# A Mamba2 block on one core: the odd tile's turned x taken from TensorE to VectorE and DRAM, its step size to ScalarE

## The reference, cut to what matters

```
xBC = silu(conv(xBC) + conv_b)          # depthwise, 4 taps
dt  = clip(softplus(dt + dt_bias), 0.001, 100)
cs  = cumsum(dt * A)                    # within a chunk
xdt = x * dt                            # per token and head
Ydiag  = einsum(scores, xdt)            # scores = (C B^T) * exp(cs_l - cs_s), lower triangle
states = einsum(B, exp(cs_last - cs), xdt)
```

## Time and profile before

| | us |
|---|---|
| median of 3 runs | 1759.31 (1758.42 to 1759.45) |
| the profiled execution, device time | 1758.21 |
| its span in the trace | 1756.4 |

### The profile page before, as it was taken

One profiled execution on the slowest core, in us unless ns is written; L12 is line 12 of the kernel. 1 busy time (PEld: TensorE's weight loads), 2 busy tenths in 40 slices (PEclk: granted clock), 3 DMA queues, 4 the chain that ended last, 5 costly groups with the idle time before them and its releaser, 6 DMA issues.

```text
span 1756.4 us, 30305 instructions
## 1 busy us (share of the span) xinstructions
PE 1742.4 (99%) x10301; PEld 1459.3 (83%) x10301; DVE 1402.7 (80%) x2211; ACT 1221.6 (70%) x2456; POOL 1232.1 (70%) x877
## 2 busy tenths in 40 slices
PE   8999999999999999999999999999999999999999
PEld 6788888888888888888888888888888888888877
DVE  7978788878878788778788788878887887868941
ACT  6986677777776777777867778767877787643320
POOL 5677777777876787677776777677777787576630
PEclk9999999999999999999999999999999999999999
DMA  5442333333333343333333333333323343236522
GB/s 196 165 131 99 116 116 112 98 123 109 134 105 94 104 135 109 108 101 117 118 102 118 116 111 108 103 109 127 123 91 103 109 135 107 76 98 175 146 78 96
DMA packets 122595, 202.84 MB, mean 115 GB/s; under 512 B 23056, under 2 KB 60560, under 8 KB 122192
## 3 DMA queue, kind: packets, MB, share of 16 engines
q1 hardware_dynamic: 120720, 197.32, 34.8%
q10 hardware_dynamic: 1728, 3.65, 0.5%
HBM read 193.57 MB, written 7.34 MB: 114 GB/s over the span
## 4 chain that ended last, share of the span: by engine, by line
PE 94%; DVE 3%; issue 1%; POOL 1%; DMA 0%; ACT 0%; SPq 0%; DVEq 0%; ACTq 0%; POOLq 0%
PE bank L143 17%; PE bank L145 16%; PE bank L144 16%; PE bank L573 10%; PE bank L609 7%; PE bank L677 7%; PE bank L679 7%; PE bank L678 6%; PE bank L888 3%; PE bank L738 3%; DVE z L1246 1%; PE bank L700 0%; DVE lm L1267 0%; PE bank L720 0%; DVE acc L1337 0%
## 5 line engine op out<-in xcount | busy, mean ns | idle before, releaser
L964 ACT ACTIVATE lm<-lm,hp 128x128 f32<-128x128 f32 x1024 | 313.1, 389 | 0.8
L1246 DVE SCALAR_TENSOR_TENSOR z<-bank,cw_all,z 128x511 f32<-128x511 f32 (+2 forms) x384 | 286.9, 747 | 13.3 <-ACT z L1000 4.2
L1611 POOL TENSOR_TENSOR conv_lo<-raw_x,conv_hi 128x512 fp32r<-128x512 f32 x124 | 203.7, 1643 | 129.4 <-ACT conv_hi L901 129.3
L143 PE MATMUL bank<-xn_hi,conv_hi 128*128 128x512 f32 x640 | 261.4, 408 | 1.9 <-DVE z L1246 1.4
L1306 DVE TENSOR_TENSOR xdt<-bank,hp 128x512 f32<-128x512 f32 x128 | 88.2, 689 | 212.4 <-PE bank L738 212.4
L145 PE MATMUL bank<-xn_hi,conv_lo 128*128 128x512 f32 x640 | 250.6, 392 | 0.0
L144 PE MATMUL bank<-xn_lo,conv_hi 128*128 128x512 f32 x640 | 249.5, 390 | 0.0
L1594 POOL TENSOR_TENSOR yt<-yt,ec 128x384 f32<-128x384 f32 x128 | 146.8, 1147 | 139.3 <-DVE ec L1315 107.9
L1280 DVE SCALAR_TENSOR_TENSOR lm<-lm,gm 128x1024 f32<-128x1024 f32 x128 | 225.3, 1760 | 7.8 <-ACT lm L964 7.2
L1578 POOL TENSOR_TENSOR y_lo<-yt,y_hi 128x512 fp32r<-128x512 f32 x128 | 180.1, 1407 | 52.4 <-ACT y_hi L1035 52.4
L143 PE MATMUL bank<-xn_hi,gate_hi 128*128 128x512 f32 x512 | 212.9, 416 | 0.0
(11 more groups left out here) (152 smaller groups left out, 4051.5 us busy)
## 6 DMA issues: line engine op xcount, KB each, us to landing
lm<-cs_d SPq DMA_DIRECT2D x128, 512.0 KB, 4.5
raw_x<-w_conv_dram SPq DMA_DIRECT2D x128, 256.0 KB, 3.5
ec<-e_d SPq DMA_DIRECT2D x256, 96.0 KB, 2.7
raw_o<-w_out_dram SPq DMA_DIRECT2D x64, 256.0 KB, 3.0
raw_g<-w_gate_dram SPq DMA_DIRECT2D x61, 256.0 KB, 3.2
raw_g<-w_conv_dram SPq DMA_DIRECT2D x16, 256.0 KB, 3.2
raw_o<-w_conv_dram SPq DMA_DIRECT2D x14, 256.0 KB, 3.4
q_raw<-w1q_dram SPq DMA_DIRECT2D x10, 256.0 KB, 3.9
```

The source lines that it names most:

```text
L143: pe.matmul(dst, a_hi, b_hi, start=(i == 0), stop=False)
L964: e = act.activation(lm[m % LM_BUFS][:, u, :], lm[m % LM_BUFS][:, u, :], ACT.Exp, bias=hp[bd.seq][:, Q_CS, k1, u:u + 1])
L1246: dve.scalar_tensor_tensor(dst[:, d:SEQ], src[:, 0:SEQ - d], cw_all[:, bd.group, pos, 3 - d:4 - d], dst[:, d:SEQ], ALU.mult, ALU.add).then ...
L1611: pool.tensor_tensor(conv_lo[kx % 2][:, :, :], raw_x[:, kx % 2, :].rearrange("p (k j) -> p k j", k=KT), conv_hi[kx % 2][:, :, :].bitcast(F ...
```

## The change

For the 59 odd tiles from 7 to 123 (`by_blocks`) x is no longer turned by TensorE. Two steps ahead VectorE transposes each 32x32 block of xt into `z[:, 1]`, SyncE writes that to a DRAM tensor `xb_d` (256 KB), and in the next step reads it back in four DMAs so that the blocks land in their turned places, in `xdt[1]`, in pieces of 32 floats. At step n VectorE makes `xw` from `xdt[1]`, and then ScalarE multiplies `xdt[1]` by dt in place, in eight operations of 128x64 with the step size as a scale per partition. `diag(n)` waits for that. Along with it `scores` of an odd step goes to the step's end, and the sum of squares of the last body from the end of step 0 to behind `y_off` of step 1.

```diff
+def by_blocks(t):
+    return paired(t) and t % 2 == 1 and t >= TILES - 1
 # SyncE
+            def blocks_out(t):
+                if by_blocks(t):
+                    sp.wait_ge(blk_done, blocks_before(t) + 1)
+                    wait(sp, xtok_in, 16 * BLK * blocks_before(t))
+                    sp.dma_start(xb_d.rearrange("g i c b j -> (g i) (c b j)"), z[:, 1, :]).then_inc(xb_out, 16)
+            def tokens_in(t):
+                if by_blocks(t):
+                    sp.wait_ge(xb_out, 16 * (blocks_before(t) + 1))
+                    sp.wait_ge(yd_done, t - 1)
+                    for b in range(BLK):
+                        sp.dma_start(xdt[1][32 * b:32 * b + 32, :].rearrange("i (c g j) -> i c g j", c=NC, g=BLK),
+                                     xb_d[:, :, :, b].rearrange("g i c j -> i c g j")).then_inc(xtok_in, 16)
                 load_rows(body, k)
+                blocks_out(n + 2)
                 ...                        # the two halves of ec
+                tokens_in(n + 1)
 # TensorE
             def diag(n, dst):
-                pe.wait_ge(xdt_done, n + 1)
+                if by_blocks(n):
+                    pe.wait_ge(xdt_act, blocks_before(n) + 1)
+                else:
+                    pe.wait_ge(xdt_done, n + 1 - blocks_before(n))
             def two_diags(body, k):
-                pe.wait_ge(xw_done, n + 1)
+                if by_blocks(n):
+                    pe.wait_ge(st_done, n)
+                else:
+                    pe.wait_ge(xw_done, n + 1)
             def turn_x(body, k):
-                if bd.exists():
+                if bd.exists() and not by_blocks(n + 1):
             def step(body, k):
                 y_off(body, k)
+                if k == 1 and body.exists():
+                    sum_squares(body, 0)
 # ScalarE
+            def weigh_x(body, k):
+                n = TILES * body.n + k
+                if by_blocks(n):
+                    act.wait_ge(xw_done, n + 1)
+                    for c in range(NC):
+                        for j in range(2):
+                            o = slice(c * P + HD * j, c * P + HD * j + HD)
+                            e = act.activation(xdt[1][:, o], xdt[1][:, o], ACT.Copy,
+                                               scale=hp[body.seq][:, Q_DT, k, NC * j + c:NC * j + c + 1])
+                    e.then_inc(xdt_act, 1)
             def raw_x_conv(body, k):
+                    if by_blocks(m - 2):
+                        act.wait_ge(xb_out, 16 * (blocks_before(m - 2) + 1))
                     work_a(body, k)
+                    weigh_x(body, k)
                     weights(body, k)
 # VectorE
+                    if by_blocks(n):
+                        dve.wait_ge(xtok_in, 16 * BLK * (blocks_before(n) + 1))
+                        dve.wait_ge(st_mm, n)
+                        dve.tensor_tensor(by_head(xw[:, :]), by_head(xdt[1][:, 0:(NC - 1) * P]),
+                                          per_token(hp[body.seq], Q_DEC, k, NC - 1), ALU.mult).then_inc(xw_done, 1)
+                    else:
                         ...                # xdt and xw from ps_x, as before
                 if pv.exists():
                     decayed()
+                if by_blocks(n + 2):
+                    dve.wait_ge(xs_done, n + 3)
+                    dve.transpose(z[:, 1, :], xt[:, (k + 2) % 4, :]).then_inc(blk_done, 1)
+                if k == 1 and before.exists() and body.exists():
+                    sums_by_token()
+                crowded = crowded or by_blocks(n)
```

More of the change, by code:

```diff
@@ L49 @@
 LM_BUFS = 4
+BLK = P // 32
 SH = 4
@@ L111, in paired, with blocks_before @@
     return TILES // 2 <= n < TILES * (BODIES - 1) + TILES // 2
+def by_blocks(t):
+    return paired(t) and t % 2 == 1 and t >= TILES - 1
+def blocks_before(t):
+    return sum(1 for u in range(t) if by_blocks(u))
 def group_exists(group):
@@ L166, in build @@
     hp_d = nc.dram_tensor("hp_d", (SEQS, P, NQ, GROUPS, TILES, 2 * NC), F32).ap()
+    xb_d = nc.dram_tensor("xb_d", (BLK, 32, NC, BLK, 32), F32).ap()
     mamba_d = nc.dram_tensor("mamba_d", (TT, P, DIM), F32).ap()
@@ L316, in build @@
         tx_done = sem("tx_done")
+        xdt_act = sem("xdt_act")
+        blk_done, xb_out, xtok_in = sem("blk_done"), sem("xb_out"), sem("xtok_in")
         xdt_done, xw_done = sem("xdt_done"), sem("xw_done")
@@ L711, in sum_squares @@
                     if body.exists():
-                        wait(pe, gev_done, TILES * body.n + k + 3)
+                        wait(pe, gev_done, TILES * body.n + 3)
                     else:
@@ L780, in step @@
                 turn_x(body, k)
-                sum_squares(body, k)
+                if not body.exists():
+                    sum_squares(body, k)
             def turn(t):
@@ L1288, in step, with sums_by_token @@
                 before = body.plus(-1)
-                if k == 1 and before.exists():
+                def sums_by_token():
                     dve.wait_ge(ss_mm, before.n + 1)
@@ L1298, in step, with decayed @@
                                       None, ALU.add).then_inc(rs_done, 1)
[L1300 to L1311, removed]
+                def decayed():
                     dve.wait_ge(yo_done, n)
@@ L1316, in step @@
                                       ).then_inc(t0_done, 1)
+                if k == 1 and before.exists() and not body.exists():
+                    sums_by_token()
+                if body.exists():
+                    if by_blocks(n):
[4 more added lines that the diff above has]
+                    else:
+                        dve.wait_ge(tx_done, n + 1 - blocks_before(n))
+                        if k == 0:
+                            wait_hp(dve, body)
+                        wait(dve, yd_done, n - 1)
+                        dve.tensor_tensor(by_head(xdt[n % 2][:, :]), by_head(ps_x[:, :]),
+                                          per_token(hp[body.seq], Q_DT, k, NC), ALU.mult).then_inc(xdt_done, 1)
+                        wait(dve, st_mm, n)
+                        dve.tensor_tensor(by_head(xw[:, :]), by_head(ps_x[:, 0:(NC - 1) * P]),
+                                          per_token(hp[body.seq], Q_DEC, k, NC - 1), ALU.mult).then_inc(xw_done, 1)
+                if pv.exists():
+                    decayed()
+                if by_blocks(n + 2):
+                    dve.wait_ge(xs_done, n + 3)
+                    dve.transpose(z[:, 1, :], xt[:, (k + 2) % 4, :]).then_inc(blk_done, 1)
+                if k == 1 and before.exists() and body.exists():
+                    sums_by_token()
                 if k == 0 and body.exists():
```

## The result

| | us |
|---|---|
| before, median of 4 runs | 1758.87 (1758.01 to 1759.45) |
| changed, median of 4 runs | 1849.83 (1847.37 to 1851.52) |
| ratio, 95% interval | 1.0514 (1.0501 to 1.0526) |
| the profiled execution, device time | 1850.88, span 1849.1 |

The change makes the kernel 91 us slower. The direction was forecast; 1811 was not, and 1850 lies outside of the range. The page's first part, against the earlier trace rows: TensorE's share falls from 99% to 95%, its busy time rises by 9 us though its stream has four transposes less in 59 tiles, and ScalarE has 112 us more.

What follows compares the result with a forecast made beforehand. TensorE, busy 99%, was taken as the bound, with ScalarE's stretch between its two waits deciding. Stalls net of removed transposes, 55.5 - 6.2 = +49, plus 3 for `scores`, gave +52 us: 1811 on the 1759.3 median; range 1788 to 1836.

Steps and rivals of the forecast that it cites:

- `diag(n)` would wait for ScalarE: By k, position of eight in a body: net +2.1 us at 3, +1.2 at 1, +0.4 at 7, -0.44 at 5.
- W: Length of ScalarE's eight `weigh_x` operations behind the exponentials: 1.97 us, taken as 2.0; bounds 1.0 and 2.45.
- the stalls of 0.84 and 1.64: TensorE's predicted waits ahead of `diag(n)` at k = 7 (0.84 us) and k = 1 (1.64 us).
- 2.55: TensorE's predicted stall ahead of `diag(n)` at k = 3, in us; net +2.1 with the transposes gone.
- The pairs of steps k = 0, 1 and 6, 7: Forecast change in length of these step pairs: +1.2 us and +0.4 us.
- Nothing was made up, nothing carried over: Claim that the stall is paid each time, as ScalarE's stretch starts anew from TensorE's clock in the next even step.
- the transpose: VectorE's 32x32 transpose, costed at nothing: between 0.69 and 1.76 us, taken as 0.7.
- signs of being wrong: Stall missing or at another k, VectorE's xw waiting for a DMA, or pairs that stall not stalling each time.
- a slide by `scores`: `scores` behind taps and state on VectorE delays the even step's chain into the k = 3 stall: 3 us (0 to 6).
- ScalarE's work behind `weigh_x` (rounding, conv copy) starts when `diag(n)` starts: Claim that this later ScalarE work adds no cost: same place at k = 3 today, 2.22 us idle later in that step.
- forecast signs: Expected in the profile after: among others, TensorE busy time down some 26 us, an eight-step body 3.3 us longer.

Runs made afterwards that it cites:

- fill_bc: Changed kernel with ScalarE's copy of C (k = 5) ahead of `weigh_x` and eight added TensorE matmuls in the k = 3 stall; 1810.33 us.
- fill_k3: Changed kernel with eight matmuls of 512 columns added at k = 3 between `diag(n-1)` and TensorE's wait for ScalarE; 1829.93 us.
- dve_weighs: Changed kernel, but VectorE multiplies `xdt[1]` by dt in one 128x512 operation behind t0 and ScalarE has no `weigh_x`; 1748.70 us.
- bc_first: Changed kernel with ScalarE's copy of the C projection (k = 5) put ahead of `weigh_x` instead of behind it; 1817.67 us.
- one_op: Changed kernel with one of ScalarE's eight multiplications by dt, seven left out; 1752.65 us.
- dve_early: dve_weighs with the four token reads issued ahead of the two ec loads of the same step instead of behind them; 1747.60 us.
- weigh_first: Changed kernel with `weigh_x` ahead of the exponentials of the same step instead of behind them; 1871.81 us.

## Why the prediction was wrong

Right: that `diag(n)` would wait for ScalarE, at k = 1, 3 and 7 and not at 5, and by how much. ScalarE's group takes 2.00 us (W was 1.97, taken as 2.0). The idle times in the middle of the pair are 0.63, 1.48 and 1.96 us by the trace (k = 7, 1, 3), 61 us in all; the stalls of 0.84 and 1.64 agree if the ends are taken by the start of the next group as in the working (953.06 - 951.33 - 0.95 = 0.78, and 977.38 - 974.80 - 0.95 = 1.63). At k = 3, 2.1 us lie in the middle and 0.3 ahead of the pair (it starts 0.64 us behind the last conv matmul, 0.32 before the change), since t0 is late behind an xw of 1.64 us; together 2.4 to 2.5, against 2.55. The pairs of steps k = 0, 1 and 6, 7 came to the forecast. Nothing was made up, nothing carried over; the transpose took 0.70 us. One of the signs of being wrong did appear: xw waits for the reads 15 times at k = 7, 22 us. It still ends 1.5 to 3 us before ScalarE starts on `weigh_x`, so it cost nothing. fill_bc, in which only this mechanism is left, takes 1810.3 against 1811. That it is so near is in part luck: 3 of the forecast's 52 us stood for a slide by `scores` that did not show, and by the pairs of steps the rest came out longer by as much.

Wrong, first: "ScalarE's work behind `weigh_x` (rounding, conv copy) starts when `diag(n)` starts. That is where it is at k = 3 today", costed at nothing. It was checked at k = 3 and taken over for all k. At k = 5 `diag(n)` does not wait for ScalarE, so everything behind `weigh_x` is simply 2 us later, and there `weights` holds the copy of C (the projection in step 4 that spares k = 5 is that of C, not of B as the prediction has it), which the gate projection needs in the same step through three taps of 2.3 us. Size: 1.4 us, 14 times, 19.6 us measured by fill_k3 against fill_bc. It was to be had from the kernel's own wait of the gate projection for the taps at k = 4 and 5.

Wrong, second: the sum took TensorE's matmuls at their length of the trace before, at full clock. After the idle time at k = 3, 2.0 us by the trace, they run at half clock, 1.5 us more in 14 bodies, 19.9 us measured by fill_k3. No rival stood for it. Before the change TensorE had no idle time of this length in the stretch, so its rows could not show what follows one; its clock was 1.000 over the whole span. The Trainium skill (TensorE: Matmul & The Clock Gate, Why this matters for your kernels) warns of idle gaps between bursts of matmuls, and was left out of the prediction; the gaps in which the clock fell here, 1.7 to 2.3 us in the changed kernel, are shorter than those that its table names.

The range went up to 1836. Its upper end held W and `scores` at their bounds, but no term for either of the two. Both were of the same kind: a consequence of the stall or of the longer ScalarE stretch outside of the chain that was worked out. Two of the forecast signs show them: TensorE's busy time went up by 9 us instead of down by 26 (in dve_weighs, with no half clock, down by 21), and a body became 6.4 us longer instead of 3.3.

Open: why the clock falls in 14 of 15 bodies of the changed kernel and in 5 of bc_first, whose stall at k = 3 is as long. In the paired steps of all ten traces the clock never fell without an idle time of at least 1.7 us beside it (fill_k3, fill_bc, one_op and dve_early have none and kept the clock). That is not enough: ten bodies of bc_first held it through the same stall, dve_weighs through one of 2.5 and weigh_first through one of 3.5. In the changed kernel the falls come 102.4 us apart, which is also the length of its body; whether that plays a part was not tried. What makes step 1 of dve_early long in every other body was seen in one timeline and not tried.

## What to carry to other kernels

An operation that is put into an engine's order delays all that stands behind it, and not only at the step where its own result is late: list each instruction behind it, in every kind of step, with who waits for it, above all where the step has slack, since there nothing masks the delay. A stall of TensorE costs more than its length if the clock falls in it; work that is thrown away can be cheaper than idleness. When an engine is 70% busy, read the stretch between its two waits for the bottleneck and not its share: VectorE at 80% could take the multiply, ScalarE at 70% could not.

## What the runs showed of the hardware

TensorE's granted clock fell to its lower level (1.2 GHz) beside idle times of 1.7 to 2.3 us in the changed kernel, and of 2.6 to 3.5 us in weigh_first, but not each time; behind those of 1.5 and 0.6 us (k = 1 and 7) it never fell. Reads of 64 KB in 512 pieces of 128 B land in 2.6 us, the four issues taking 2.63 us of SyncE's queue together; the wait for them at k = 7 cost nothing. xw from SBUF takes 0.54 to 1.71 us, where it took 0.55 from PSUM. The long ones, 32 of 59, all overlap an operation of GpSimd by 1 us or more, here y_lo: it runs for 2.27 us where its median before was 1.29, and xw ends 0.4 us behind it (998.12 against 997.71). That the overlap makes both long is read from such rows and was not tried.

```profile
971.04 0.56 DVE L1368 TENSOR_TENSOR xw<-xdt,hp 128x384 f32<-128x384 f32 x1
...
996.48 1.64 DVE L1368 TENSOR_TENSOR xw<-xdt,hp 128x384 f32<-128x384 f32 x1
```
```profile
995.44 2.27 POOL L1649 TENSOR_TENSOR y_lo<-yt,y_hi 128x512 fp32r<-128x512 f32 x1
```
